# Attention scores from stacked bf16 parts, loaded from DRAM, in place of f32 scores on zero-padded heads

## What is computed

```python
normed = layer_norm(x, gamma1, beta1)
qkv = normed.reshape(b_, n_, H, HD).transpose(0, 2, 1, 3)        # H = 8, HD = 16
scores = jnp.einsum('bhqd,bhkd->bhqk', qkv, qkv) * scale
masked = jnp.where(adj_matrix[:, None, :, :] > 0, scores, -jnp.inf)
attn = jax.nn.softmax(masked, axis=-1)
out = jnp.einsum('bhqk,bhkd->bhqd', attn, qkv)
x = x + out.transpose(0, 2, 1, 3).reshape(b_, n_, d_)
```

## Time and profile before

| | us |
|---|---|
| median of 3 runs (lowest to highest) | 3308.82 (3308.73 to 3311.3) |
| the profiled execution | 3315.0 |
| its span, first to last instruction | 3312.9 |
| attention, from its first load to its last add | 44.83 to 716.44 |
| first scores of the first group | 65.33 |

### The profile page before, as it was taken

One profiled execution on the slowest core, in us unless ns is written; L12 is line 12 of the kernel. 1 busy time (PEld: TensorE's weight loads), 2 busy tenths in 40 slices (PEclk: granted clock), 3 DMA queues, 4 the chain that ended last, 5 costly groups with the idle time before them and its releaser, 6 DMA issues. The chain is left out here.

```text
span 3312.9 us, 81916 instructions
## 1 busy us (share of the span) xinstructions
PE 2953.5 (89%) x26275; PEld 2586.8 (78%) x26402; DVE 2091.8 (63%) x6992; ACT 1629.6 (49%) x3020; POOL 1383.2 (42%) x1961
## 2 busy tenths in 40 slices
PE   3999999979989999999999987888862999997998
PEld 2999999979977777777777766777762999997787
DVE  4777777757766666666666654888873545443332
ACT  0444444435546666666666653555541444443443
POOL 2333333323322323232322222777773666665332
PEclk7999999989999999999999997887875999999999
DMA  1111111100000000000000000111142222221333
GB/s 37 42 42 38 38 38 39 40 11 0 0 1 0 0 0 0 0 0 0 0 0 0 0 2 28 56 53 55 56 127 68 77 77 77 77 81 56 111 104 89
DMA packets 166260, 126.10 MB, mean 38 GB/s; under 512 B 24246, under 2 KB 149689, under 8 KB 166202
## 3 DMA queue, kind: packets, MB, share of 16 engines
q1 hardware_dynamic: 148794, 89.43, 10.1%
q0 software_dynamic: 17408, 35.95, 3.2%
HBM read 68.36 MB, written 48.56 MB: 35 GB/s over the span
## 5 line engine op out<-in xcount | busy, mean ns | idle before, releaser
L780 POOL TENSOR_TENSOR s_sw<-s_expo,s_rsum 128x512 f32<-128x512 f32 x128 | 133.4, 1042 | 605.5 <-DVE s_rsum L1026 605.5
L1763 ACT ACTIVATE e_hidden<-e_ps,e_b1g 128x512 f32<-128x512 f32 x288 | 194.5, 687 | 257.6 <-PE e_ps L61 256.4
L394 ACT ACTIVATE a_prob<-a_prob 128x1024 f32<-128x1024 f32 x128 | 135.3, 1057 | 367.6 <-DVE a_prob L488 367.6
L1741 POOL DMA_INDIRECT token_y<-e_y,e_rows x288 | 282.5, 981 | 78.0 <-issue 68.3
L1226 POOL DMA_INDIRECT sorted_z<-r_z,r_rows x256 | 250.4, 978 | 84.9 <-issue 84.3
L1797 PE MATMUL e_ps<-expert_w,e_hidden 128*128 x2304 | 280.2, 275 | 0.0
L1797 PEld LDWEIGHTS e_ps<-expert_w,e_hidden 128*128 128x128 f32 x2304 | 273.8, 192 | 6.3
L434 PEld LDWEIGHTS a_ps_s<-a_headT,a_nT 128*128 128x128 f32 x2048 | 270.6, 193 | 8.7
L434 PE MATMUL a_ps_s<-a_headT,a_nT 128*128 128x128 f32 x2048 | 271.8, 276 | 0.0
L459 PEld LDWEIGHTS a_ps_o<-a_V,a_probT 128*128 128x128 f32 x2048 | 242.1, 194 | 0.8 <-issue 0.8
L459 PE MATMUL a_ps_o<-a_V,a_probT 128*128 128x17 f32 x2048 | 241.0, 260 | 0.7 <-DVE a_attn L479 0.7
(11 more groups left out here) (344 smaller groups left out, 8065.4 us busy)
## 6 DMA issues: line engine op xcount, KB each, us to landing
e_z<-sorted_z SPq DMA_DIRECT2D x72, 260.0 KB, 3.0
c_y<-token_y SPq DMA_DIRECT2D x32, 512.0 KB, 3.9
X<-in_x_dram SPq DMA_DIRECT2D x32, 256.0 KB, 2.9
a_adj<-in_adj_dram SPq DMA_DIRECT2D x32, 256.0 KB, 3.2
a_headT<-a_nT SPq DMA_DIRECT2D x256, 32.0 KB, 2.0
g_adj<-in_adj_dram SPq DMA_DIRECT2D x32, 256.0 KB, 2.9
out_dram<-X SPq DMA_DIRECT2D x32, 256.0 KB
token_y<-e_y,e_rows POOLq DMA_INDIRECT x288, 2.3
```

Source lines behind the costliest of these rows:

```text
L1741: nc.gpsimd.indirect_dma_start(sh.token_y, bass.IndirectOffsetOnAxis(ap=rows[p][:, b:b + 1], axis=0), y[p][:, b, :], None).then_inc(y_scat ...
L1763: nc.scalar.activation(hidden[p][:, c, :], ps_1[c % 2][:, :], ACT.Gelu, bias=b1g[p][:, c:c + 1]).then_inc(s["hidden_done"], 1)
```

## The change

It rewrites `attention_phase`. nT is split into three bf16 parts (high, middle, rest) with the columns of the features in the order (d h). The parts go to a DRAM tensor `terms` in one store for each group, and come back as two stacks of 96 rows: `left` and `right` hold the blocks of 16 rows whose six products add up to the f32 product. Each stack is loaded in two halves of two graphs, and each half by three transfers (STACKS), in rows of 4096 bytes. The scores are then bf16 products over 96 rows, made twice: once with the row's node on the partitions, for the row maximum, and once transposed, with the maximum (split in three, turned by PE, and put by a small transfer under `right`) subtracted by three more rows. The exponential therefore gives probT at once; the subtraction on DVE, the eight turns and the copies of them go. The last product has V as the weight (17 columns) and probT moving (128 columns), writes four heads side by side at partitions 0, 32, 64 and 96, and is copied and turned back by PE. ACT writes X1 instead of DVE. gcol and bcol, the gammas in the new order, are loaded by 32 small transfers at the start. LAG goes from 3 to 4 (6 for SP) and PEEL from 4 to 6.

```diff
+        STACKS = ((0, 3), (3, 2), (5, 1))
+        K, PARTS, HALF = 6 * HD, 3, 2 * T
+        split = two("a_split", [D, 3, 2, HALF], BF16)
+        left, right = (two(f"a_{n}", [K + PARTS, 2, HEADS, HALF], BF16) for n in ("left", "right"))
+        terms = [nc.dram_tensor(f"a_terms{i}", [3, 2, HD, HEADS, HALF], BF16, kind="Internal").ap() for i in range(2)]
+        ps_s, ps_st = ps("a_ps_s", [T, HEADS, T]), ps("a_ps_st", [T, HEADS, T])
...
 SP:
-                for h in range(HEADS):
-                    rows = slice(h * HD, (h + 1) * HD)
-                    sp.dma_start(headT[1 - p][rows, h, :], nT[1 - p][rows, :]).then_inc(headT_loaded[1 - p], 16)
+            for d in range(HD):
+                for tile, gamma in ((gcol, norm["gamma1"]), (bcol, norm["beta1"])):
+                    sp.dma_start(tile[d * HEADS:(d + 1) * HEADS, :], gamma.rearrange("(h d) -> h d", d=HD)[:, d:d + 1],
+                                 allow_slow_non_contiguous=True).then_inc(s["columns"], 16)
+            def stack(own, half):
+                for term, (block, n) in enumerate(STACKS):
+                    rows = slice(block * HD, (block + n) * HD)
+                    sp.dma_start(left[own][rows, half, :, :],
+                                 terms[own][term:term + 1, half, :, :, :].to_broadcast([n, HD, HEADS, HALF]))\
+                      .then_inc(ab_loaded[own][half], 16)
+                    sp.dma_start(right[own][rows, half, :, :],
+                                 terms[own][0:n, half, :, :, :].rearrange("t d h n -> t d (h n)"))\
+                      .then_inc(ab_loaded[own][half], 16)
+            def step(t, r, p, known):
+                for b in range(GB):
+                    if live(kk, 1, n_graphs):
+                        sp.wait_ge(s["maxT_done"], k)
+                        sp.dma_start(right[own][K:K + PARTS, i // 2, :, (i % 2) * T:(i % 2 + 1) * T],
+                                     topsT[(b + 1) % 2][:, :]).then_inc(max_loaded[(b + 1) % 2], 16)
+                    if b == 0 and live(known, 2, groups):
+                        sp.wait_ge(s["st_done"], t * 4 - 12)
+                        stack(p, 1)
+                    if b == 1: (load of X for t + 1)
+                    if b == 2: (load of adj for t)
+                    if b == 2 and live(known, 1, groups):
+                        sp.wait_ge(s["split_done"], t)
+                        sp.dma_start(terms[q].rearrange("t a d h n -> (d h) (t a) n"),
+                                     split[q][:, :, :, :].rearrange("p t a n -> p (t a) n")).then_inc(stored[q], 16)
+                    if b == 3 and live(known, 1, groups):
+                        sp.wait_ge(s["st_done"], t * 4 - 10)
+                        sp.wait_ge(stored[q], (r + p) * 16)
+                        stack(q, 0)
...
 POOL, for each graph (four small operations, each waiting for the one before):
+                        nc.gpsimd.tensor_tensor(own[:, 0, :], top[b % 2][:, :], zero[:, :], ALU.add)
+                        nc.gpsimd.tensor_tensor(top_rest[:, :], top[b % 2][:, :], own[:, 0, :], ALU.subtract)
+                        nc.gpsimd.tensor_tensor(own[:, 1, :], top_rest[:, :], zero[:, :], ALU.add)
+                        nc.gpsimd.tensor_tensor(own[:, 2, :], top_rest[:, :], own[:, 1, :], ALU.subtract)
...
 PE, for each graph:
+                        (wait ab_loaded[p][0] at b == 2, ab_loaded[q][1] at b == 0, top_done of the graph before)
+                                last = nc.tensor.matmul(ps_s[:, h, :], left[own][0:K, half, h, cols],
+                                                        right[own][0:K, half, h, cols], ...)
+                        nc.tensor.matmul(ps_m[:, 0:T], tops[(b + 1) % 2][:, :, :], sh.ident_bf[:, :], ...)
+                        (wait max_loaded of the graph three slots back)
+                                last = nc.tensor.matmul(ps_st[:, h, :], left[own][:, half, h, cols],
+                                                        right[own][:, half, h, cols], ...)
+                            last = nc.tensor.transpose(ps_o[:, c, :], oT[(b + 1) % 2][:, c, :], sh.ident[:, :])
-                            last = nc.tensor.transpose(ps_p[:, h, :], prob[(b + 1) % 2][:, h, :], sh.ident[:, :])
-                            last = nc.tensor.matmul(ps_o[:, h, :], probT[b % 2][:, h, :],
-                                                    own[:, (b + 2) % GB, h, :], start=True, stop=True)
+                            at = 32 * (h % 4)
+                            last = nc.tensor.matmul(ps_ot[at:at + HD + 1, h // 4, :], V[own][:, i, h, :],
+                                                    probT[b % 2][:, h, :], start=True, stop=True)
...
 ACT:
-                        nc.scalar.activation(prob[b % 2][:, :, :], prob[b % 2][:, :, :], ACT.Exp, ...)
-                            last = nc.scalar.activation(probT[(b + 1) % 2][:, 4 * c:4 * c + 4, :], ps_p[...], ACT.Copy)
+                        nc.scalar.activation(topsT[(b + 1) % 2][:, :], ps_m[:, 0:T], ACT.Copy)
+                        nc.scalar.activation(probT[(b + 1) % 2][:, :, :], ps_st[:, :, :], ACT.Exp, ...)
+                        nc.scalar.activation(oT[b % 2][:, :, :], ps_ot[:, 0:2, :], ACT.Copy)
+                        (for each group: split[q][:, 0] beside nT, and the four X1 of L505)
...
 DVE:
-                        nc.vector.tensor_tensor(prob[b % 2][:, :, :], ps_s[b % 2][:, :, :], top..., ALU.subtract)
-                        (for each group: the four X1 of L505)
+                        (for each group: nT - split 0, the copy to split 1, nT - split 1 into split 2)
```

More of the change, by code:

```diff
@@ L251, in attention_phase @@
+        K, PARTS, HALF = 6 * HD, 3, 2 * T
+        adj = two("a_adj", [T, GB, T], I32)
+        edge_bias = two("a_edge_bias", [T, GB, T], BF16)
         stats = sb("a_stats", [T, GB, 6])
[L252 to L264, removed]
@@ L284, in attention_phase @@
[L284 to L294, removed]
+        max_loaded = [sem(f"a_max_loaded{i}") for i in range(2)]
@@ L296, in attention_phase @@
+        ab_loaded = [[sem(f"a_ab_loaded{i}{j}") for j in range(2)] for i in range(2)]
+        stored = [sem(f"a_stored{i}") for i in range(2)]
+        AB = 16 * 2 * len(STACKS)
         block = ctx.enter_context(nc.Block())
@@ L298, in attention_phase, with graph @@
         adj_g = adj_in.rearrange("(g b) n d -> g n b d", b=GB)
-        LAG, PEEL = 3, 4
+        LAG, PEEL = 4, 6
+        def graph(t, b, known):
+            return None if known is None else (known - 2) * GB + b - 2, (t - 2) * GB + (b - 2)
         @block.sync
         def _(sp):
[L305 to L321, removed]
-                for h in range(HEADS):
-                    rows = slice(h * HD, (h + 1) * HD)
-                    sp.dma_start(headT[1 - p][rows, h, :], nT[1 - p][rows, :]).then_inc(headT_loaded[1 - p], 16)
[L325 to L331, removed]
@@ L333, in _ @@
+            run_steps(sp, step, groups - 2, LAG + 2, PEEL)
         @block.gpsimd
         def _(pool):
[L335 to L338, removed]
-            def step(t, r, p, known):
[L341 to L356, removed]
-                for b in range(GB):
[L359 to L363, removed]
@@ L396, in step @@
                     if live(kk, 1, n_graphs):
[L397 removed]
+                        act.wait_ge(s["max_turned"], k)
                         if since(kk, 3):
[L399 to L403 removed]
@@ new lines, in step @@
+                        nc.scalar.activation(topsT[(b + 1) % 2][:, :], ps_m[:, 0:T], ACT.Copy).then_inc(s["maxT_done"], 1)
+                    if live(kk, 3, n_graphs):
+                        act.wait_ge(s["st_done"], k - 2)
+                        if since(kk, 5):
+                            act.wait_ge(s["pv_done"], k - 4)
+                        nc.scalar.activation(probT[(b + 1) % 2][:, :, :], ps_st[:, :, :], ACT.Exp,
+                                             scale=float(HD) ** -0.5).then_inc(s["prob_done"], 1)
@@ new lines, in step @@
+                    if b == 0 and live(known, 1, groups):
+                        act.wait_ge(s["n_turned"], t)
+                        if since(known, 2):
+                            act.wait_ge(s["split_done"], t - 1)
+                        if since(known, 3):
+                            for half in range(2):
+                                act.wait_ge(ab_loaded[q][half], (r - 1 + p) * AB)
+                        nc.scalar.activation(nT[:, :], ps_n[:, :], ACT.Identity, bias=bcol[:, 0:1],
+                                             scale=gcol[:, 0:1])
+                        nc.scalar.activation(split[q][:, 0, :, :], ps_n[:, :], ACT.Identity, bias=bcol[:, 0:1],
+                                             scale=gcol[:, 0:1]).then_inc(s["nT_done"], 1)
@@ new lines, in step @@
+                    if b == 1 and live(known, 0, groups):
+                        dve.wait_ge(s["stats_done"], t + 1)
+                        if since(known, 2):
```

(6 more changed lines are left out.)

376 lines of the change are left out of this document (240 added, 136 removed).

## The result

The changed kernel takes 3589.2 us (median of 4 runs, 3586.09 to 3596.57) against 3308.78 us (3308.35 to 3311.3): a ratio of 1.0849, 95% interval 1.083 to 1.0868. That is 280 us slower; 334 were forecast (3643 us). Of the profiled execution the span is 3585.4 us, 272.5 more than before.

A forecast was written before the change was run, and what follows sets the result against it. PE bounds the kernel before; afterwards confined loads and the store chain make 30 us a group: 31 x (30 - 19.95) = +311, +17 start, +6 end, on 3315.0 gives 3649, median 3643 us; range 3160 to 3720.

The forecast's parts named there:

- PE's own work: Attention phase, PE after the change: scores, V product and turns sum to 3.3 us a graph, 13.2 a group (12 to 19).
- PE gains little: Rival: strips do not overlap, bf16 weights load like f32; 19.5 us a group, about 3308 us, no change; chance 0.04.
- The loads: Stack transfers confined by outermost counts 3 and 2: 541 KB, 22.5 us on the busiest engine, 26.4 with small transfers; chance 0.74.
- the two bounds: Rate of one DMA engine on stack rows: 25.75 GB/s at best, 21.2 on average for long packets; 24 taken.
- The chain behind the store: Next stack issued only after the group's store landed: busy engines idle some 3.5 us a group (0 to 5).
- The small transfers behind the stacks: The maximum waits in the queue behind half a stack (11 us), stopping PE; no cost beyond the period.
- The clock: PE, idle half of each group, at 1.2 GHz needs at most 26 us, under 30; nothing charged.
- Start and end: Ends of the attention phase: first scores near 82 us instead of 65.33, +17; longer pipeline at the end, +6.
- The rival with hidden loads: Stack loads spread over all or changing engines and hidden: about 3174 us (3130 to 3260); chance 0.22.
- the pace goes to POOL and PE: Step of the hidden-loads rival: with loads hidden, POOL and PE set 15.2 us a group (13.8 to 18).
- The load at which the cases part: Busiest engine's load under which loads would be hidden: some 16 us at 24 GB/s, given as 390 KB instead of 541.

The follow-up runs named there:

- runs 1 to 3: Changed kernel with the feature index outermost in all stack transfers, in the 48-row ones alone, in the 32-row ones alone: 3273.37, 3363.37 and 3368.28 us.
- run 4: Changed kernel with stacks loaded from DRAM tensors stored once by the first two groups, so none waits for its own group's store: 3555.44 us, ratio 1.0737.
- run 5: Changed kernel with the four small transfers of the maximum per group issued by ACT on their own queue instead of by SP behind the stacks: ratio 1.0796.
- run 1: Changed kernel with the feature index outermost in all six transfers of a half stack, same bytes, rows and waits: 3273.37 us, ratio 0.9889.
- Runs 10 to 12: On top of run 1: PE's turn of the maximum later; that plus POOL's split before its addition; the split alone: ratios 0.9725, 0.966, 0.9766.

## Why the prediction was right, step by step

- **PE's own work.** Forecast 3.3 us a graph. The timeline of a warm slot of the changed kernel:

```profile
525.13 0.63 PE L553 MATMUL a_ps_ot<-a_probT,a_V 128*17 128x128 f32 x16
...
525.70 0.39 PE L501 MATMUL a_ps_s<-a_edge_bias,ident_bf 128*128 128x512 bf16 x1
...
525.92 0.39 PE L505 MATMUL a_ps_s<-a_right,a_left 96*128 96x128 bf16 x4
...
526.15 0.38 PE L501 MATMUL a_ps_s<-a_edge_bias,ident_bf 128*128 128x512 bf16 x1
```

  The granted clock from 525.0 to 526.6 us is 1.00. Four bf16 products take 0.23 us (525.92 to 526.15), 0.057 each: 0.06 was taken. The sixteen records of the last product take 0.57 us (525.13 to 525.70), 0.036 each, where 1.0 us was taken and 1.71 was the upper end. The strips at different partitions overlap: a product takes a third of the 0.107 us of the earlier trace rows. With this PE's work is smaller than forecast, 3.3 - 0.4 = 2.9 us a graph; it had no part in the result, since the loads set the pace. The rival "PE gains little" falls with this. By the Trainium skill ("TensorE: Matmul & The Clock Gate", Part 3) such products run at once; the trace agrees.
- **The loads.** Right in cause and size. Stack rows are in flight for 23.5 us of a group, where 22.5 was forecast for the busiest engine; smaller packets alone for 3.0 us, where 3.4 and 0.5 were. A row runs at 25.8 GB/s, the upper of the two bounds (24 was taken), so that the 132 rows of the busiest engine alone are 21.0 us; the other 2.5 us are the spread of the durations, the third engine and gaps between the transfers, not told apart here. The rule of the Trainium skill ("DMA: Bandwidth & Descriptors", "Rules for kernel authors") that an outermost dimension under 16 confines a DMA to that many engines holds here for 3 and for 2: in runs 1 to 3 the number of late steps is none, two and three. That the same engines serve both counts is shown by the changed kernel, where two steps are late and not five; which engines of the sixteen they are, no trace here tells.
- **The chain behind the store.** 3.5 us forecast; the time without a packet is 1.8 us a group, and taking the wait away brought 1.0 (run 4). This is the mis-sized term: 31 x 2.5 = 78 us too much, of which 31 x 0.9 = 28 came back in the load (27.34 against 26.4). I had the queue run dry from the end of the store's data to the first row of the next stack; the store lands 6.8 us after issue but SP, late itself, waits only 1.2 us of this. For the profiled executions the difference is -62 us (3649 forecast, 3587.1 measured): the pace -52, the end of the phase -8, the start +1, behind the phase -2. The median is off by -54 only because it lies 2 us above the profiled execution and not 6 below; these 8 us are luck.
- **The small transfers behind the stacks** cost nothing beyond the period: run 5.
- **The clock.** PE idles between bursts, and the granted clock of the stretch is 0.77, a mix of both levels (1.2 and 2.4 GHz); at 58% busy it stays hidden, as forecast.
- **Start and end.** First scores +18.0 us, +17 forecast, and that is partly luck: the terms written there add up to 59 + 2 + 3 + 13 = 77 us, and 82 was given. In the trace SP issues the last small load at 55.2 us (they take 0.29 us and not 0.40), the store at 66.2, the first stack at 68.9, and the scores start at 83.3. The 11 us from the loads to the store, which hold all of nT's making, were put down as 2. At the end 277 from pace and start against 274.9 measured: -2, +6 forecast.
- **The rival with hidden loads** named the right mechanism and the wrong pace. It gave 3174 us from a period of 15.2; run 1, which is that case made real, has 19.04 and 3273. The step that failed is "the pace goes to POOL and PE": I added up POOL's 14 us and charged 1.2 us for uneven slots. In fact POOL's split of the maximum stands behind the deviation, PE's order puts its turn right behind the scores, and the wait costs 3.0 us, after which PE runs a slot at the lower level of the clock (the 0.63 us above). Runs 10 to 12 bring up to 2.4 us back without touching a single duration; the rest to 15.2 was not found. (The load at which the cases part, given there as 390 KB, is 384 by its own working, 24 GB/s x 16 us; nothing hangs on it.)

## What to carry to other kernels

Before sizing a DMA by its bytes, look at the outermost index of both sides: a transfer of 192 KB in rows of 4 KB went over three engines or over all of them by the order of two indices, and a mean DMA share of 0.28 hid two engines that had work for nearly the whole group. The signs in a profile are a transfer elsewhere in the queue whose landing time has grown several times over (2.9 to 13.6 us), and long rows of low digits in the DMA slices; if the trace has the steps of a transfer's semaphore, the number of late ones is the number of busy engines. And a period worked out from sums of busy time was here a lower end (15.2 against 19.04 us): where an engine's order puts a long block ahead of a short result that another engine waits for, the order sets the pace.

## What the runs showed of the hardware that was not expected

- The issue of a transfer on SP is itself slower behind a stack. In the changed kernel, the same transfer of 128 KB in the first half and, with the first half still under way, in the second:

```profile
522.72 0.61 SPq L319 DMA_DIRECT2D a_right<-a_terms  x1
...
528.12 2.62 SPq L319 DMA_DIRECT2D a_right<-a_terms  x1
```

  It takes 0.61 us to issue or 2.62; over the phase the medians are 0.61 and 2.3, and in run 1, with as many transfers and bytes, every issue of a stack takes 0.4 to 0.6. That the queue is full at this point would explain it; no run shows that.
- A row of 4096 bytes takes 0.159 us (25.8 GB/s) when two or three are in flight, and 0.293 us (14.0 GB/s) in run 1, where mostly sixteen are. So spreading the stacks brought the time with a stack row in flight from 23.5 to 8.3 us a group, and not to the 3.8 us of 24 rows for each engine at 0.159.
- Two chips ran the same attention phase alike (19.04 us a group on both) and a later stage at a granted clock of 0.82 and 0.73 (2000 to 2300 us); the whole program differs by 4%.
